# Where the routing of a mixture of experts stands: scatters, second counts, the list of tiles and the row weights moved in a seam of a four-layer kernel

## The reference

```python
def _L3_ffn_ref(hidden_states, ...):
    x = hidden_states.reshape(-1, H)                      # 2048 tokens
    w, sel = _route(x, gate_weight, expert_bias)          # sigmoid scores + bias; 2 of 4 groups; best 4 experts
    out = _moe(x, w, sel, gate_proj, up_proj, down_proj)  # sum over chosen experts of w * (silu(x g) * (x u)) d
    shared = silu(x @ shared_gate.T) * (x @ shared_up.T) @ shared_down.T
    return out + shared

def _L2_ffn_ref(x, ...):
    aff = sigmoid(x wa); topk_p, topk_i = top_k(aff, 2)   # best 2 of 16 experts
    return x + shared + routed
```

## Time and profile before

| | us |
|---|---|
| median of 3 runs (1430.29 to 1447.88) | 1431.4 |
| the profiled execution, its own time | 1438.35 |
| its span | 1436.6 |
| PE busy (share of span) | 1144.2 (80%) |
| DVE busy | 781.3 (54%) |
| POOL busy | 565.3 (39%) |
| ACT busy | 502.0 (35%) |

### The profile page before, as it was taken

How to read it: one execution, slowest core, us unless ns; L and a number is a source line. 1 busy time by engine, 2 the same in 40 slices (tenths; PEclk the granted TensorE clock), 3 DMA queues, 4 the chain that set the end, 5 groups by cost and what they waited for, 6 DMA issues and landing times. The chain is left out here.

```text
span 1436.6 us, 25477 instructions
## 1 busy us (share of the span) xinstructions
PE 1144.2 (80%) x7228; PEld 822.1 (57%) x7229; DVE 781.3 (54%) x2794; ACT 502.0 (35%) x1336; POOL 565.3 (39%) x854
## 2 busy tenths in 40 slices
PE   5377975499999993799986889967996786699970
PEld 4255764287777772466655766624554444577750
DVE  5857434222444444687845545576777634655547
ACT  0254210012333330466652134413674431144430
POOL 4651056500333333665562324412221556355550
PEclk9998887599999996899998899956999956899995
DMA  9599932201333337111010224344000112255547
GB/s 398 153 301 287 340 120 87 76 16 33 106 108 107 106 102 288 60 48 57 2 43 30 80 77 135 105 143 172 1 2 1 47 65 88 87 148 151 147 136 263
DMA packets 92378, 169.37 MB, mean 118 GB/s; under 512 B 11287, under 2 KB 70825, under 8 KB 91305
## 3 DMA queue, kind: packets, MB, share of 16 engines
q1 hardware_dynamic: 72585, 107.63, 24.4%
q0 software_dynamic: 17664, 48.91, 9.5%
q10 hardware_dynamic: 2043, 11.75, 2.0%
HBM read 82.64 MB, written 85.61 MB: 117 GB/s over the span
## 5 line engine op out<-in xcount | busy, mean ns | idle before, releaser
L2071 PE MATMUL bank<-weights,xT 128*128 x832 | 241.4, 413 | 1.9 <-ACT xT L2159 1.7
L1914 POOL DMA_INDIRECT slots_out<-weights,y_rows x128 | 122.7, 959 | 166.1 <-DVE y_rows L2313 105.7
L2071 PEld LDWEIGHTS bank<-weights,xT 128*128 128x128 f32 x832 | 142.4, 191 | 27.8 <-issue 4.0
L1908 POOL DMA_INDIRECT slots_in<-xn_wide,row_in x114 | 112.4, 986 | 113.7 <-DMA slots_in<-xs_wide 50.8
L1914 POOL DMA_INDIRECT slots_out<-pack,y_rows x80 | 76.5, 956 | 194.8 <-DVE y_rows L2313 186.2
L2159 ACT COPY xT<-bank 128x256 f32<-128x256 f32 x208 | 77.5, 373 | 120.8 <-PE bank L2063 100.6
L1403 PE MATMUL bank<-ctx,weights 32*128 32x256 f32 x512 | 78.4, 448 | 37.5 <-DVE weights L1511 22.3
L2013 PE MATMUL bank<-weights,rows 128*128 128x256 f32 x256 | 75.2, 413 | 34.9 <-DVE x L2263 18.5
L1457 ACT ACTIVATE weights<-bank 128x512 f32<-128x512 f32 x128 | 72.6, 597 | 71.3 <-PE bank L1411 66.1
L2255 DVE TENSOR_TENSOR rows<-rows,bank 128x256 f32<-128x256 f32 (+1 forms) x56 | 22.5, 401 | 137.5 <-ACT rows L2141 109.7
L2290 DVE TENSOR_TENSOR weights<-weights,bank 128x128 f32<-128x128 f32 x128 | 36.8, 287 | 109.8 <-ACT weights L2163 98.5
(11 more groups left out here) (418 smaller groups left out, 2543.5 us busy)
## 6 DMA issues: line engine op xcount, KB each, us to landing
slots_in<-xs_wide SPq DMA_DIRECT2D x16, 2112.0 KB, 19.0
weights<-slots_in SPq DMA_DIRECT2D x96, 132.0 KB
xs_wide<-slots_in SPq DMA_DIRECT2D x72, 132.0 KB
rows<-slots_out SPq DMA_DIRECT2D x16, 512.0 KB, 3.4
xn_wide<-slots_out SPq DMA_DIRECT2D x16, 512.0 KB, 4.8
weights<-in_l_gu SPq DMA_DIRECT2D x1, 7040.0 KB
pack<-slots_in SPq DMA_DIRECT2D x40, 132.0 KB
weights<-in_l_gu ACTq DMA_DIRECT2D x1, 4608.0 KB, 14.5
```

What stands on the lines that cost most here:

```text
L1908: pool.indirect_dma_start(out=slots_in, in_=xn_wide[:, t, :], in_offset=None, out_offset=bass.IndirectOffsetOnAxis(ap=row_in[:, t, i:i + 1 ...
L1914: pool.indirect_dma_start(out=slots_out, in_=y[:, n % U, :], in_offset=None, out_offset=bass.IndirectOffsetOnAxis(ap=y_rows[:, n % U:n % U ...
L2071: last = nc.tensor.matmul(out, xT[:, n.c % 2, c, :], flat(gu_w[:, ds(e, 1), c, :]), start=(c == 0), stop=(c == C - 1 and layer != 2))
```

## The change

Four edits, two of them in both mixtures.

- Channel heads: the second group's count moves from batch 15 to batch 16; the second group's routing takes one piece per step instead of two; the 32 scatters at b = 13 to 18 become 36 at b = 13 to 17, with 14 at b = 15 and none at b = 18. The mixture's late scatters fall from 16 to 12.
- Mixture 2: the count comes at chunk 3 instead of 2, with three pieces per chunk instead of five.
- Mixture 3: the whole choice is done ahead of the first chunk, the count comes at chunk 1 instead of 2.
- Mixtures 2 and 3: `weigh_rows` moves from ahead of `tiles_listed` to behind the last shared add.

```diff
-            count_in = (11, 15)
-            scatter_in = {13: 6, 14: 6, 15: 6, 16: 6, 17: 4, 18: 4}
+            count_in = (11, 16)
+            scatter_in = {13: 6, 14: 6, 15: 14, 16: 6, 17: 4}
...
-                        for _ in range(g + 1):
-                            next(routing[g], None)
+                        next(routing[g], None)
...
-                                              2: (((t0, NB),), (0,), (2,), 5), 3: (((t0, NB),), (0,), (2,), 4)}[layer]
+                                              2: (((t0, NB),), (0,), (3,), 3), 3: (((t0, NB),), (0,), (1,), 4)}[layer]
...
                         yield from list_tiles(layer, dve, step, rt)
-                        yield from weigh_rows(layer, dve, step, rt)
+                        if layer == 1:
+                            yield from weigh_rows(layer, dve, step, rt)
                         dve.sem_inc(tiles_listed, 1)
...
+                if layer == 3:
+                    for _ in choice[0]:
+                        pass
                 for n in range(len(chunks) + 3):
...
                 for _ in placement[-1]:
                     pass
+                for _ in weigh_rows(layer, dve, step, rt) if layer > 1 else ():
+                    pass
...
-            mixture(3, rt, carve, LAST, scattered, 16)
+            mixture(3, rt, carve, LAST, scattered, 12)
```

## The result

| | kernel before | changed kernel |
|---|---|---|
| median of 4 runs, us | 1431.89 (1430.29 to 1447.88) | 1454.92 (1451.26 to 1458.67) |
| profiled execution, its span | 1438.35, 1436.6 | 1451.26, 1449.5 |
| mixture 2: DVE's first instruction, first routed tile | 765.88, 835.69 | 767.32, 838.18 |
| mixture 3: the same | 1186.31, 1248.90 | 1203.56, 1267.37 |
| last stretch, first tile of mixture 3 to the end of the span | 187.7 | 182.1 |

The ratio is 1.0127, with a 95% interval of 1.0083 to 1.0171. The block of mixture 3 begins 17.25 us later: 1.4 of that stood already ahead of mixture 2, where nothing was edited, 1.1 came in mixture 2 up to its first tile, and 14.8 between that tile and the block.

The account below looks back on a forecast made before the run. The pace of PE, ACT and DVE through the shared expert, with DVE also routing, bounds the tiles' start. Mixture 2's 7 us plus mixture 3's 5 (heads' 7.7 loss deducted) gave 12 us earlier: 1420 us, range 1406 to 1436.

Parts of the forecast that it names:

- mixture 2, block to first tile: Mixture 2's shared expert: routing ends so that the product of chunk 9 comes 7 us earlier, bounds 3 and 8.
- weights of mixture 2: Between mixture 2's last add and first product: 2.76 us of weights fill DVE's idle 2.73 us and cost nothing.
- heads, b = 14: Channel heads, batch 14: pieces of choice move behind the add PE waits for, 2 us earlier, between 1.3 and 3.
- heads, b = 15 and the train of 14: Channel heads, batches 15 and 16: a 1.1 us count leaves 15 and returns behind the logits, zero in sum.
- count and placing, then roots behind scatters: End of the heads: late count and placing, roots queued behind scatters on POOL; mixture 3's block begins 7.7 us later.
- mixture 3 without spells: Mixture 3, block to routed tiles: they can start 41 us into the block if no engine is starved.
- dry spells: Mixture 3: engines getting instructions singly or not at all during POOL's scatter trains; taken as 6 us, bounds 0 and 24.
- weights of mixture 3: Behind mixture 3's last add: weights take 5.5 us where DVE idled 2.52, so 3.0 us stay on the path.
- a decision point of 18: Mixture 3: from 18 us of dry spells on, they decide against the change (11 gained without any, and 7).
- the starved seam: Rival, chance 0.16: mixture 3's scatters join into one train of some 28, 24 us of dry spells, time 1437.
- signs of being wrong: Mixture 3's block no later; mixture 2's first tile after 832; mixture 3's "remote" gaps over 18 us, or none.
- the case that I had built on the rule: Rival, chance 0.17: mixture 2 gives only 2 to 3 us, time 1425; or dry spells gone, 0.22, time 1411.

Follow-up runs that it names:

- e5_after: The changed kernel itself run again in a fed session, against the kernel before: 1341.73 us, ratio 0.9949.
- e4_none: The changed kernel without the 28 scatters that mixture 3 issues itself, fed session: 1342.51 us, ratio 0.9936 to the kernel before.
- f2_none3: The changed kernel with none of the 64 scatters of layer 3, starved session: 1405.2 us, ratio 0.9791 to the kernel before.
- e7_roots: The changed kernel with the second group's 8 scatters of the heads moved behind the last roots, fed session: 1338.97 us, ratio 0.9916 to the kernel before.
- e1_heads: The kernel before with the edits of the channel heads alone, fed session: 1352.95 us, ratio 1.0028.
- h2_four: f3_woven with mixture 1's 64 scatters in fours, POOL waiting for shared-expert chunks ahead of each, starved session: 1400.94 us, ratio 0.9595 to the kernel before.
- f3_woven: Kernel before plus both mixtures' edits, 36 head scatters, mixture 3's weights made one slot per chunk between DVE's last adds; starved: 1429.91 us, ratio 0.9948.

## Why the prediction was wrong, step by step

| Step | forecast, us | measured, us | where |
|---|---|---|---|
| mixture 2, block to first tile | -7 | +1.1 | 69.8 to 70.9, starved |
| the same, fed | | -3 to -6 | 68.8 or 68.9 to 65.8 or 62.8 |
| weights of mixture 2 | 0 | 0 | idle 0.18 for 2.73 |
| heads, b = 14 | -2 | -0.9 | add of batch 13 |
| heads, b = 15 and the train of 14 | -1 | +6.6 | add of batch 14 |
| count and placing, then roots behind scatters | +10.7 | +9.8 | next block against that add |
| mixture 3 without spells | 41 | 40.8, 40.3, 40.5 | e5_after, e4_none, f2_none3 |
| dry spells in mixture 3 | 6 | 23 | 63.8 less 40.8 |
| weights of mixture 3 | +3.0 | +2.5 | PE's wait at 1273.07 |
| last stretch, with these weights in it | +3.0 | -5.6 | 187.7 to 182.1 |

*What bounds the kernel.* Right. In every trace the first tile follows the last add, or the load behind the last scatter, and that fits the forecast's saying that raising `tiles_listed` is worth nothing by itself.

*The failed step* is "I take 6" for the dry spells of mixture 3. I had the right account of them (14 us before, an upper bound of 24, a decision point of 18) and chose a value near the lower end by an argument that the trace did not carry: that a spell costs what lies between the choice and the end of its train. That argument also let the late scatters run on from the last roots at 1190.5; but POOL has to pass the end of the block like the others, and the train began with the block, at 1204.14. So the choice was through before any spell, and placing and list were hit. In both kernels a spell starts some nine to thirteen scatters into a train and lasts to its end or a few us longer. So a long train without a pause is what to look for. The change made or moved three, of which the forecast had 6 us for the third and nothing for the others: 14 scatters in one go at b = 15 where there were six (+6.6, and 7.6 against the forecast), a train moved onto the products of mixture 2 (8 us against the forecast, of which 5 lie between this kernel's 70.9 starved and 65.8 fed), and the two trains of mixture 3 joined into one of 28 (+17). I had seen the last one and called it the starved seam, at 0.16 and 24 us; it came with 23. For b = 15, DVE's wait in the changed kernel, starved and then fed (e5_after):

```profile
1176.51 0.26 DVE L1526 RECIPROCAL weights<-bank 128x16 f32<-128x16 f32 x1 [15.07 <-PE bank L1372]
```
```profile
1091.29 0.26 DVE L1526 RECIPROCAL weights<-bank 128x16 f32<-128x16 f32 x1 [7.61 <-PE bank L1372]
```

Two of the forecast's own signs of being wrong came true: the first tile of mixture 2 later than 832 (838.18), and more than 18 us of gaps named "remote" in mixture 3 (12.08, 8.00 and 7.91 on ACT). The sum of the steps would have been worse than the 12.9 us between the spans, had the last stretch not come out 8.6 better than forecast.

*Mixture 2.* The working (pieces moved, weights hidden) holds in direction where engines are fed: 62.8 us in the runs in which PE's clock was granted 0.74 in the first 10 us of the block (between its two levels of 1.2 and 2.4 GHz), 65.8 where it was 0.59, and the changed kernel itself is of the second sort, 3 us of gain where 7 were forecast. "In mixture 2 a train of 18 scatters shows no such gap" misread the trace: the gaps of 9.87 us on ACT and 4.85 us on DVE, shown above, end at that train's end. They fell where PE had work; the old order took 69.8 us starved and 68.8 or 68.9 fed.

*The roots' wait* was named, queued behind the right scatters and sized to 1 us: the forecast's 7.7 without the 3 us that it took off up to the logits is 10.7, and 9.8 came. But the scatters ahead of the roots are only half of it. Without them the block begins 16.81 (e7_roots) or 16.18 us (f2_none3) behind the add of batch 14, with them 20.94 or 21.73, before the change 11.93. So 4 to 5.5 us are the scatters, and the rest is the late count, behind which L1577 of batch 14 now stands on DVE; the forecast's path ran through both and did not say that the second alone would hold the roots. Freed from the scatters, the fed kernel gained 2.8 in the median; these scatters then ended later (PE waited 6.99 us for its first load in e7_roots).

*The last stretch* is 5.6 us shorter in the changed kernel (187.7 to 182.1), where the forecast had it 3.0 longer for the weights. In fed sessions it is 2.6 longer (179.5 in e1_heads, 182.1 in e5_after), near the 2.5 us that PE waits for them. In starved ones it ran from 180.7 to 187.7 over the kernels; this I leave open.

*The rule that I weighed* (the Trainium skill, Runtime: NRT & Kernel Launch, Instruction fetch mechanics: refills by a DMA of their own, "mostly hidden"). Nothing in the fed sessions speaks against it; in the starved ones the gaps came back in the changed seam, and the case that I had built on the rule did not come. Whether refills have to do with it the runs do not show. The profiles of a starved and of a fed run have the same two rows for the instruction queues, here of the changed kernel in its starved session:

```profile
q8 instruction: 46, 0.75, 0.2%
q14 instruction: 40, 0.33, 0.1%
```

What a train of scatters takes from the other engines, and why only in some sessions, stays open.

*The range* of 1406 to 1436 missed by 19. It was built on the bounds of mixture 2 and 0 to 14 us of dry spells, and reached only a little way into the starved case. The spells alone were worth 23, and both further trains could be read off POOL's changed order.

## What to carry to other kernels

Price a stretch by who is fed in it, not only by who is busy: gaps named "issue" or "remote" on several engines at once, inside one engine's long train of issues, are a resource of their own. Count each train's length without a pause, and treat an edit that lengthens, joins or moves one as if it added work. Where such a train has slack, let it wait for the progress of the work beside it every four issues: together with the mixtures' edits, 12 late scatters and the woven weights this gave 57 and 66 us in starved sessions, and no loss showed in fed ones (0.9900 and 0.9896 with the waits, 0.9914 with the mixtures' edits alone; the same kernel without its waits was not run fed, so their own cost is not measured). And a profile from one session may show a machine state and not the kernel; a term that rests on gaps without a releaser needs a second session.

## What the runs showed of the hardware that was not expected

- The same kernel takes 1349 to 1351 us in some sessions and 1432 to 1458 in others, on the same chip too, with nearly the same DMA share (0.29, and 0.28 to 0.29) and POOL pace (1.26 us per scatter). The difference is that PE, ACT and DVE stand idle, mostly without a releaser, while POOL issues indirect scatters: 28 matmuls in 20 us against 102. Why is not shown.
- Trains of 4 to 12 with pauses of 1.3 to 3.6 us between them nearly remove it: PE 16.52 and 20.00 busy of 20 us in h2_four, instead of 5.11 and 6.66 in f3_woven.
- A starved PE loses twice: its granted clock was 0.50 in the second of those windows and 1.00 in the fed run and in the one with the waits. Of its two levels that is 1.2 against 2.4 GHz.
